# The first block of a weight fold: its opening piece loaded as two sets of 64 rows, one copy moved from VectorE to ScalarE

## The reference

```
h   = x @ W.T + b + 2.0 * (x @ A[slot]) @ B[slot]          # a LoRA pair of rank 16 for each batch
y   = h @ W2.T + b2                                         # base of the second layer
res = h @ A2.T          # 64 wide
p   = softmax(h @ router.T)     # 16 experts, the best two kept, weights made to sum to one
out = x + y + 0.5 * sum_e p[e] * (res @ B2[e].T)
```

## Time and profile before

| | |
|---|---|
| median of 3 runs | 101.38 us (101.21 to 102.25) |
| the profiled execution | 101.33 us, span of its instructions 99.5 us |
| TensorE matmuls | 95.6 us busy, 572 instructions |
| VectorE, ScalarE, GpSimd busy | 66.6, 41.5, 22.2 us |
| mean TensorE clock granted | 0.998 |

### The profile page before, as it was taken

The page is one execution under the profiler, slowest core; times in us unless marked ns, Lnnn a source line. Parts: engine busy times, 40 slices in busy tenths (PEclk is TensorE's granted clock), DMA queues, the critical chain, the costliest instruction groups (busy, mean ns, idle before and its releaser), DMA issues.

```text
span 99.5 us, 1810 instructions
## 1 busy us (share of the span) xinstructions
PE 95.6 (96%) x572; PEld 87.0 (87%) x572; DVE 66.6 (67%) x184; ACT 41.5 (42%) x101; POOL 22.2 (22%) x34
## 2 busy tenths in 40 slices
PE   6799999999999999999999999999999999999990
PEld 6699999999999999998898799888787877878980
DVE  5669996997485885899977567257949275572101
ACT  3514636968787546756522610451334022040000
POOL 4100004224999965108123000000000000000000
PEclk9999999999999999999999999999999999999999
DMA  1999659999558675891780836516228074020211
GB/s 42 331 326 410 207 123 361 267 361 352 150 91 205 203 239 151 232 231 37 221 253 25 214 119 163 153 43 184 106 76 255 26 194 122 0 105 0 105 59 53
DMA packets 8379, 16.91 MB, mean 170 GB/s; under 512 B 1507, under 2 KB 4067, under 8 KB 8370
## 3 DMA queue, kind: packets, MB, share of 16 engines
q1 hardware_dynamic: 7762, 16.41, 55.1%
q10 hardware_dynamic: 576, 0.39, 1.2%
q0 software_dynamic: 32, 0.00, 0.0%
HBM read 13.28 MB, written 2.16 MB: 155 GB/s over the span
## 4 chain that ended last, share of the span: by engine, by line
PE 93%; DMA 3%; DVE 0%; ACT 0%; issue 0%
PE pair L820 90%; DMA w_raw_all<-w_cat 3%; PE pair L965 1%; PE pair L967 1%; PE pair L985 1%; DVE xn L814 0%; ACT w_hi_all L420 0%; PE pair L955 0%; PE pair L944 0%; PE pair L942 0%; PE pair L934 0%
## 5 line engine op out<-in xcount | busy, mean ns | idle before, releaser
L820 PE MATMUL pair<-e_hi,w_hi_all 128*128 128x512 f32 (+1 forms) x72 | 27.1, 376 | 0.0
L820 PE MATMUL pair<-e_hi,w_lo_all 128*128 128x512 f32 (+1 forms) x72 | 26.7, 370 | 0.0
L820 PE MATMUL pair<-e_lo,w_hi_all 128*128 128x512 f32 (+1 forms) x72 | 26.7, 370 | 0.0
L533 ACT ACTIVATE w_hi_all<-exp_raw_all 128x512 fp32r<-128x512 f32 x16 | 9.7, 630 | 15.3 <-DVE exp_raw_all L755 15.3
L820 PEld LDWEIGHTS pair<-e_hi,w_lo_all 128*128 128x128 f32 x72 | 13.6, 188 | 2.5
L820 PEld LDWEIGHTS pair<-e_hi,w_hi_all 128*128 128x128 f32 x72 | 13.6, 188 | 2.5
L820 PEld LDWEIGHTS pair<-e_lo,w_hi_all 128*128 128x128 f32 x72 | 13.6, 189 | 2.0
L762 DVE TENSOR_TENSOR w_lo_all<-exp_raw_all,w_hi_all 128x512 fp32r<-128x512 f32 x16 | 10.4, 689 | 4.5 <-ACT w_hi_all L533 4.0
L755 DVE TENSOR_TENSOR exp_raw_all<-w_raw_all 128x512 f32<-128x512 f32 x16 | 11.2, 741 | 0.1
L769 DVE TENSOR_TENSOR xn<-pair,xn 128x512 f32<-128x512 f32 x7 | 4.8, 690 | 8.9 <-PE pair L820 8.9
L820 PE MATMUL pair<-p_hi,x_hi 128*128 128x304 f32 x32 | 10.0, 311 | 0.0
(11 more groups left out here) (107 smaller groups left out, 162.2 us busy)
## 6 DMA issues: line engine op xcount, KB each, us to landing
w_raw_all<-spill SPq DMA_DIRECT2D x16, 256.0 KB, 4.2
xt_raw<-x_t SPq DMA_DIRECT2D x4, 512.0 KB, 6.3
exp_raw_all<-experts SPq DMA_DIRECT2D x4, 512.0 KB, 8.7
xn<-x_n SPq DMA_DIRECT2D x4, 512.0 KB, 5.8
out<-xn SPq DMA_DIRECT2D x7, 256.0 KB, 2.8
w_raw_all<-w_cat SPq DMA_DIRECT2D x2, 552.0 KB, 6.4
c_stack<-c_hi SPq DMA_DIRECT2D x7, 74.0 KB, 3.9
c_stack<-c_lo SPq DMA_DIRECT2D x7, 74.0 KB, 4.2
```

Of the source, the lines that this page charges most:

```text
L533: nc.scalar.activation(gt_hi[:, t % 2, js, :], g[:, js, :], ACT.Copy).then_inc(gh_done, 1)
L820: return nc.tensor.matmul(out_ap, lhs, rhs, start=first, stop=last)
```

## The change

It reorders chunk 0. The right half of the first factor (W_RIGHT) is now the leading half, with output blocks m = 2, 3 first; W_LEFT comes second. W_RIGHT and W2_LEFT are neighbours in a row, so that LEAD, their 552 columns, is one run of 2,208 bytes. It is loaded by two DMAs on the same semaphore: rows 0 to 63 by SP, rows 64 to 127 by ScalarE; both ScalarE and VectorE wait for 32. Then SP loads W2_RIGHT and ScalarE loads W_LEFT, 128 rows each, as before. The high part of W2_RIGHT is made by ScalarE, between its copies of W_RIGHT and W_LEFT, and no longer by VectorE. The counts of `wh_first` in later waits fall by one.

```diff
+W_LEAD, W_REST = W_RIGHT, W_LEFT
+LEAD = slice(W_LEAD.start, W2_LEFT.stop)
...
-            for n, cols in enumerate((W2_LEFT, W2_RIGHT)):
-                sp.dma_start(w_raw[:, 0, cols], w_cat[0, :, cols]).then_inc(in_w2_side[n], 16)
+            sp.dma_start(w_raw[0:P // 2, 0, LEAD], w_cat[0, 0:P // 2, LEAD]).then_inc(in_lead, 16)
+            sp.dma_start(w_raw[:, 0, W2_RIGHT], w_cat[0, :, W2_RIGHT]).then_inc(in_w2_right, 16)
...
-            for n, cols in enumerate((W_LEFT, W_RIGHT)):
-                act.dma_start(w_raw[:, 0, cols], w_cat[0, :, cols]).then_inc(in_w_side[n], 16)
-            act.wait_ge(in_w_side[0], 16)
-            for cols in (slice(0, P), slice(P, 2 * P)):
-                nc.scalar.activation(w_hi[:, 0, cols], w_raw[:, 0, cols], ACT.Copy).then_inc(wh_left, 1)
-            act.wait_ge(in_w_side[1], 16)
-            nc.scalar.activation(w_hi[:, 0, W_RIGHT], w_raw[:, 0, W_RIGHT], ACT.Copy).then_inc(wh_done, 1)
+            act.dma_start(w_raw[P // 2:, 0, LEAD], w_cat[0, P // 2:, LEAD]).then_inc(in_lead, 16)
+            act.dma_start(w_raw[:, 0, W_REST], w_cat[0, :, W_REST]).then_inc(in_rest, 16)
+            act.wait_ge(in_lead, 32)
+            for cols in (slice(2 * P, 3 * P), slice(3 * P, 4 * P)):
+                nc.scalar.activation(w_hi[:, 0, cols], w_raw[:, 0, cols], ACT.Copy).then_inc(wh_lead, 1)
+            act.wait_ge(in_w2_right, 16)
+            nc.scalar.activation(w_hi[:, 0, W2_RIGHT], w_raw[:, 0, W2_RIGHT], ACT.Copy).then_inc(wh_right, 1)
+            act.wait_ge(in_rest, 16)
+            nc.scalar.activation(w_hi[:, 0, W_REST], w_raw[:, 0, W_REST], ACT.Copy).then_inc(wh_done, 1)
...
-            first_block_hi(0, W2_LEFT)
+            dve.wait_ge(in_lead, 32)
+            nc.vector.tensor_copy(w_hi[:, 0, W2_LEFT], w_raw[:, 0, W2_LEFT]).then_inc(wh_first, 1)
             dve.wait_ge(wh_first, 1)
             first_block_lo(W2_LEFT, wl_first)
-            dve.wait_ge(wh_left, 2)
-            first_block_lo(W_LEFT, wl_done)
-            first_block_hi(1, W2_RIGHT)
-            dve.wait_ge(wh_first, 2)
+            dve.wait_ge(wh_lead, 2)
+            first_block_lo(W_LEAD, wl_done)
+            dve.wait_ge(wh_right, 1)
             first_block_lo(W2_RIGHT, wl_first)
             dve.wait_ge(wh_done, 1)
-            first_block_lo(W_RIGHT, wl_done)
+            first_block_lo(W_REST, wl_done)
...
-            for half, rows_done in enumerate((wh_left, wh_done)):
-                ms = range(half * KC // 2, (half + 1) * KC // 2)
+            for half, rows_done in enumerate((wh_lead, wh_done)):
+                ms = range((1 - half) * KC // 2, (2 - half) * KC // 2)
...
-                    pe.wait_ge(wh_first, side + 1)
-                    for m in ms:
-                        pe.wait_ge(rows_done, 1 if half else m + 1)
+                    pe.wait_ge(wh_right if side else wh_first, 1)
+                    for n, m in enumerate(ms):
+                        pe.wait_ge(rows_done, 1 if half else n + 1)
```

More of the change, by code:

```diff
@@ L177, in adaln_ffn_kernel @@
         in_w = [None] + [sem(f"in_w{k}") for k in range(1, KC)]
-        in_w_side = [sem("in_w_left"), sem("in_w_right")]
-        in_w2_side = [sem("in_w2_left"), sem("in_w2_right")]
+        in_lead = sem("in_lead")
+        in_rest = sem("in_rest")
+        in_w2_right = sem("in_w2_right")
         in_w_next = sem("in_w_next")
@@ L194, in adaln_ffn_kernel @@
         wh_first = sem("wh_first")
-        wh_left = sem("wh_left")
+        wh_lead = sem("wh_lead")
+        wh_right = sem("wh_right")
         wh_next = sem("wh_next")
@@ L597, in _ @@
             nc.vector.memset(low_row[F_BIAS:F_BIAS + 1, :], 0.0).then_inc(first_set, 1)
-            def first_block_hi(n, cols):
-                dve.wait_ge(in_w2_side[n], 16)
-                nc.vector.tensor_copy(w_hi[:, 0, cols], w_raw[:, 0, cols]).then_inc(wh_first, 1)
             def first_block_lo(cols, done):
@@ L619, in _ @@
                 nc.vector.tensor_copy(w_hi[:, k, D:], w_raw[:, k, D:]).then_inc(wh_first, 1)
-                dve.wait_ge(wh_first, k + 2)
+                dve.wait_ge(wh_first, k + 1)
                 nc.vector.tensor_tensor(w_lo[:, k, D:], w_raw[:, k, D:], w_hi[:, k, D:].bitcast(F32),
@@ L852, in _ @@
             for k in range(1, KC - 1):
-                pe.wait_ge(wh_first, k + 2)
+                pe.wait_ge(wh_first, k + 1)
                 for n, m in enumerate((2, 3, 0, 1) if k == 1 else range(KC)):
@@ L872, in _ @@
             pe.wait_ge(wh_done, KC)
-            pe.wait_ge(wh_first, KC + 1)
+            pe.wait_ge(wh_first, KC)
             pe.wait_ge(wl_first, KC + 1)
```

## The result

The changed kernel is slower: 103.42 us median (101.78 to 104.38, 22 runs) against 101.78 for the kernel before beside it (101.12 to 102.76, 22 runs). The forecast was 101.2 us, range 100.9 to 101.8. The profiled execution after took 103.66 us (span 101.9), 2.33 us more than the one before.

What follows compares the result with a forecast made beforehand. TensorE, busy 96%, bounds the kernel, so only the fold's start and block 0's holes count. Chunk 1 at 7.80 instead of 7.95 takes 0.15 us off 101.33, giving 101.18; median 101.2 us, range 100.9 to 101.8.

Steps and rivals of the forecast that it cites:

- The step on T: Opening load: fewer, longer pieces lift the slow first microsecond, so T is taken as 3.7 instead of 3.9.
- T: Moment both halves of the opening piece are in; taken as 3.7 us, bounded between 3.3 and 4.5.
- Small terms at nothing: Effects priced at zero: SP's later loads up to 0.2 us later after 64-row issues, hidden by chunk 1's slack.
- The second rival: Opening, first copies: later half sets T past 3.9, costing T - 3.9; 101.7, bound 102.0; slower by 0.1 to 0.6, chance 0.20.
- the third rival's chain: ScalarE's queue: table loads 0.2 us or more later delay chunk 1's copy; 101.3; chance 0.30 shared with nothing moving.
- its 0.15 us to TensorE: Before chunk 1: TensorE may start about 0.15 us after ScalarE's copy ends, 7.65 giving 7.80.
- the 0.2 us allowed: SP's queue: loads after its 64-row first issue, chunk 1's included, may go out up to 0.2 us later.
- T - 3.9: Second rival's price: every term of block 0 hangs on T, so lateness past 3.9 us counts in full.
- Part 2: Block 0: right piece's copy moves from VectorE to ScalarE, closing two TensorE holes; chunk 1 starts at T + 4.06.
- its cases: Forecast gain 0.1 to 0.25 us, 0.45; within 0.1, 0.30; slower by 0.1 to 0.6, 0.20.
- The ceiling of 0.25 us for a gain: Chunk 1's start: ScalarE's copy without delay allows 7.70 instead of 7.95, so at most 0.25 us.
- the copy at 7.13: ScalarE's copy for chunk 1, starting at 7.13 in the old profile; with 0.1 us delay it ends at 7.65.

Runs made afterwards that it cites:

- ScalarE's chain without the gap: Changed kernel with 17 instead of 13 matmuls on zeros: 103.27 us against 101.88 for the kernel before, ratio 1.0143.
- the gap without the chain: Kernel before with 10 instead of 13 matmuls on zeros, nothing else changed: 103.46 us against 101.82, ratio 1.0169.
- W_LEFT repaired alone: Changed kernel with W_LEFT's load issued by SP, third in its queue ahead of chunk 1: 103.28 us against 101.9 for the kernel before.
- both repairs together: Changed kernel with W_LEFT's load third on SP and 17 matmuls on zeros: 102.14 us against 101.82 for the kernel before, ratio 1.0045.
- the loads by columns: Changed kernel with the opening loaded by columns of 128 rows again, copy still on ScalarE: 101.55 us against 101.88 before; repeated, 101.81 against 101.82.
- the one load of 128 rows: Changed kernel with the 552-column opening piece as one load of 128 rows from SP: 101.47 us against 101.88 for the kernel before, ratio 0.9971.

## Why the prediction was wrong

**What bounds the kernel, and where the change acts.** Right: all of the loss came in before chunk 1, the rest of the span shifted with it.

**The step on T failed.** I took T = 3.7, with the argument that fewer, longer pieces would lift the slow first microsecond. T was 4.4 in the profile after and 4.0 to 4.25 in the five other kernels with a half on each queue. A row that hinted at it was there: 64-row issues of 0.45 to 0.60 us. I used it only under "Small terms at nothing", for SP's later loads, and never for the opening itself. It would have told a part at most: the issue was 0.16 us longer, and ScalarE's half took 3.6 us to land instead of 3.2. The second rival had the right mechanism, that the slower of the two halves sets T, and priced this part rightly: T = 4.4 gives 0.5 us, and TensorE started 0.51 us late. Its upper bound was 102.0 all the same, since T was all it had.

**The landings of the second loads were taken over from before.** The whole part on ScalarE rests on the second loads of the two queues being in at 4.4 and 4.5. W_LEFT came at 7.3; W2_RIGHT, on SP, at 4.8. That made the third rival's chain (last copy, table loads, chunk 1's copy) a matter of 2.5 us instead of 0.05 to 0.2. I had the chain, its order and its 0.15 us to TensorE right, and looked for the delay in the added copy, which caused none: with the same copy and loads of 128 rows chunk 1's copy ran at 6.94. SP's part of chunk 1 was later too, issued at 1.98 instead of 1.66 and in at 7.5 instead of 6.6, more than the 0.2 us allowed; the chain on ScalarE hid it.

**The clock was not in the working at all.** I read TensorE's 0.55 us of idleness before the fold as time that costs itself. In the run with 10 matmuls on zeros, 1.05 us there came with a loss of 1.64 us in the median. A later T is therefore not worth T - 3.9, as the second rival said, but that plus, in many runs, a chunk 0 at the lower clock.

**The parts do not add.** ScalarE's chain without the gap costs 1.4 us, the gap without the chain 1.6 (before with 10), W_LEFT repaired alone gives back 0.1 to 0.3 us in the median, and both repairs together bring 103.4 to 102.1. Both delays hold up the same moment, chunk 1's start, and the later one decides.

**Part 2 was right in its mechanism**, as the repairs show it: VectorE's second copy went, its four subtracts stood back to back once W_LEFT was in time, and the copy on ScalarE cost nothing. At the fast pace and with the halves kept, chunk 0's sixth pair of matmuls started 1.69 us behind the fold with the copy moved (4.62 to 6.31, W_LEFT's load on SP) and 1.85 with the copy left on VectorE (4.71 to 6.56): a hole of 0.16 us that the move closes, in one profile of each. The gain of up to 0.25 us is within what two measurements could not confirm (0.9963, then 0.9999).

**What the forecast allowed for.** The prediction gave 0.05 to everything outside its cases and 0.04 to a loss of over 1%, and wrote that a move by a microsecond would be explained by none of its working. That is what came. The range ended at 101.8, below the 102.0 that its own bound on T gave. The ceiling of 0.25 us for a gain was not tested, as no version was faster beyond the noise; and the copy at 7.13 that it hangs on was not fixed, since it ran at 6.94 with the loads by columns and at 6.70 with the one load of 128 rows.

## What to carry to other kernels

Splitting a load changes its issue and can change what stands behind it on the same queue (here ScalarE's, hardly SP's), so give every later load of that queue a landing time of its own and do not take it from the old trace. Keep opening loads at 128 rows unless a run shows otherwise. And count TensorE's idleness ahead of its first real work twice: once for itself, and once for the clock that may stay low after it; two delays that meet at the same point must both be repaired before either repair shows.

## What was not expected of the hardware

An issue of 64 rows took 0.57 us against 0.41 for 128 rows of the same queue, with pieces of 2,208 and of 1,184 bytes alike. SP's first traffic then came after 2.05 us instead of at 1.75 to 1.80, in all eight kernels that had a half at the head of SP's queue. ScalarE's first traffic behind its own half came at 2.5 to 2.75 us instead of at 1.9 to 2.05, in six. The issue of 128 rows right behind a half was long too: 0.56 us on SP against 0.41, and 0.84 on ScalarE against 0.46. Why all this is so is open.

A load of 128 KB on ScalarE's queue landed in 2.4 us as its first beside halves on SP, in 3.2 and 3.4 as its first beside one load of 128 rows, in 3.3 as the second behind a load of 128 rows (the kernel before), and in 5.3 to 5.9 as the second behind a half of 64 rows. On SP the same place was not slow: W2_RIGHT's load behind a half took 3.0 to 3.4 us against 3.2 before, and W_LEFT's as the third 3.4 and 3.7. Why the one on ScalarE's queue took so long was not settled.

The moment at which TensorE went from 1.2 to 2.4 GHz differed much. With 13 matmuls on zeros the trace's record has it at 3.62 us (0.55 us of idleness before the fold), 4.05 to 4.22 (0.73 to 0.85 us), 5.18 to 6.48 (0.26 to 0.31 us) and 9.46 (1.46 us); with 15 and no listed wait at 6.80, with 17 at 4.15 and 4.71, with 10 and 1.05 us at 9.91. These are single profiles. Up to 0.85 us of idleness they show no order; the three profiles with 0.98 us or more all had most of chunk 0 at the lower level, and no run with 10 matmuls on zeros was as fast as the median of before.
